# Local attention of the gate stage in blocks of 64 queries with 128 keys each, a tile of two blocks at a step, and outputs divided by the sums instead of weights

## What is computed

```python
h = shift_token(x)
q, k, v = split(h @ wqkv)                 # 8 heads of 64
q, k = l2norm(q) * qs, l2norm(k) * ksc
q, k = rotary_xpos(q, k)
bq = q.reshape(b, h, w, 64, d) * 8.0
bk, bv = look_around(k), look_around(v)   # the block before and the own: 128 keys
sim = einsum('bhwid,bhwjd->bhwij', bq, bk)
mask = (i < j) | (i > j + 64) | (j == -1)
attn = softmax(where(mask, -max, sim))
out = einsum('bhwij,bhwjd->bhwid', attn, bv)
x = x + out @ wo
h = layernorm(shift_token(x)) * lg + lb
a, g = split(h @ w1 + b1)
x = x + (a * gelu(g)) @ w2 + b2
```

## Time and profile before

| | us |
|---|---|
| median of 3 runs | 5320.43 |
| lowest, highest | 5319.44, 5322.79 |
| the profiled execution | 5323.64 |
| its span, first to last instruction | 5322.3 |
| PE busy in the span | 4695.6 (88%) |
| DVE busy | 3288.0 (62%) |
| ACT busy | 2561.0 (48%) |
| POOL busy | 2385.0 (45%) |

### The profile page before, as it was taken

One profiled execution on the slowest core, in us unless ns is written; L12 is line 12 of the kernel. 1 busy time (PEld: TensorE's weight loads), 2 busy tenths in 40 slices (PEclk: granted clock), 3 DMA queues, 4 the chain that ended last, 5 costly groups with the idle time before them and its releaser, 6 DMA issues. The chain is left out here.

```text
span 5322.3 us, 68694 instructions
## 1 busy us (share of the span) xinstructions
PE 4695.6 (88%) x27244; PEld 2291.9 (43%) x27244; DVE 3288.0 (62%) x4302; ACT 2561.0 (48%) x3877; POOL 2385.0 (45%) x1387
## 2 busy tenths in 40 slices
PE   5999999978888688876979999996799999999997
PEld 3444444435556333332423222222445555555554
DVE  4756565637777677684067777855266655655564
ACT  2344444446665355553236666661244444444443
POOL 0455555557666177784010000000046666666675
PEclk8999999989999799897979999997799999999998
DMA  0000000010000000000000000000000000000000
GB/s 32 3 3 3 3 3 4 1 36 9 9 9 1 3 1 2 2 1 23 0 4 1 2 1 2 1 1 8 9 3 3 1 3 3 3 2 2 3 1 9
DMA packets 52289, 27.81 MB, mean 5 GB/s; under 512 B 30036, under 2 KB 48256, under 8 KB 51712
## 3 DMA queue, kind: packets, MB, share of 16 engines
q1 hardware_dynamic: 51968, 23.42, 1.7%
HBM read 22.36 MB, written 1.05 MB: 4 GB/s over the span
## 5 line engine op out<-in xcount | busy, mean ns | idle before, releaser
L793 DVE TENSOR_REDUCE L_part<-banks 128x2 f32<-128x1024 f32 (+2 forms) x1600 | 1882.3, 1190 | 996.4 <-PE banks L644 856.1
L778 ACT ACTIVATE L_weights<-banks 128x1024 f32<-128x1024 f32 (+1 forms) x1600 | 1580.4, 1000 | 1051.5 <-PE banks L676 837.9
L702 PE MATMUL banks<-L_weights,L_V 128*32 128x512 f32 (+3 forms) x6400 | 1500.9, 605 | 5.1 <-ACT L_weights L778 3.0
L1000 POOL TENSOR_TENSOR L_wsum<-L_wsum,L_weights 128x1024 f32<-128x1024 f32 (+1 forms) x448 | 987.2, 2204 | 55.2 <-ACT L_weights L778 2.5
L983 POOL TENSOR_TENSOR L_wsum<-L_wsum,L_two 128x1024 f32<-128x1024 f32 x240 | 570.4, 2377 | 859.1 <-DVE L_two L967 856.3
L702 PEld LDWEIGHTS banks<-L_weights,L_V 128*64 128x64 f32 (+1 forms) x6400 | 283.7, 123 | 460.0 <-issue 397.9
L676 PE MATMUL banks<-L_QH,L_KH 64*128 64x512 f32 (+3 forms) x1664 | 432.2, 453 | 18.1 <-issue 10.2
L2488 POOL MEMSET F_xr<- 128x16 f32 x1 | 0.1, 125 | 932.5 <-POOLq L97 932.5
L644 PE MATMUL banks<-L_KH,L_QH 64*128 64x512 f32 (+3 forms) x1664 | 371.0, 428 | 30.4 <-ACT L_weights L778 17.4
L676 PE MATMUL banks<-L_QL,L_KH 64*128 64x512 f32 (+3 forms) x1664 | 372.3, 382 | 0.0
L676 PE MATMUL banks<-L_QM,L_onesrow 64*128 64x512 f32 (+3 forms) x1664 | 371.6, 381 | 0.0
(11 more groups left out here) (447 smaller groups left out, 6375.9 us busy)
## 6 DMA issues: line engine op xcount, KB each, us to landing
F_tab<-xpos SPq DMA_DIRECT2D x8, 512.0 KB, 4.0
F_h<-L_ffn_h_w SPq DMA_DIRECT2D x2, 1024.0 KB, 7.0
F_wqkv<-L_ffn_wqkv SPq DMA_DIRECT2D x2, 768.0 KB
L_cos<-rope_cos SPq DMA_DIRECT2D x1, 1024.0 KB, 5.0
L_sin<-rope_sin SPq DMA_DIRECT2D x1, 1024.0 KB, 7.1
...
```

What stands on the lines that cost most here:

```text
L702: mm = pe.e.matmul(O[r, c:BANK], self.V[g % 2][:, kt, h, :], self.W[x % self.NW][:, y, c:BANK], start=kt < starts, stop=kt >= tiles - starts)
L778: act.e.activation(self.W[x % self.NW][:, :, c:BANK], self.banks(it)[:, :, c:BANK], ACT.Exp, scale=self.scale).then_inc(self.exped, 1)
L793: dve.e.tensor_reduce(self.part[n % 3][:, pr, j, p, :], self.banks(it)[:, :, 0:wide], AX.X, ALU.max).then_inc(self.mx_read, 1)
L1000: pool.e.tensor_tensor(acc[:, :, c:BANK], acc[:, :, c:BANK], W[:, :, c:BANK], ALU.add).then_inc(self.summed, 1)
```

## The change

A tile's attention is now one step of two half steps, for all eight heads. A tile holds two blocks of 64 queries, and each block is multiplied with its own 128 keys only, so that a score tile has 128 columns of keys for each head instead of 256. The tile of scores has the same two banks, now for 8 heads.

- score: the mask is 128 by 128, read four times over for each bank (2 matmuls a tile instead of 4). The scores are 16 matmuls a tile, each of 64 rows by 64 columns of weights with 128 keys streamed; before they were 8 with 128 columns of weights and 256 streamed.
- exp: 8 exponentials of 128 columns a tile, instead of 8 of 256.
- wturn: 8 transposes a tile instead of 16, straight from the undivided weights.
- values: 16 matmuls a tile as before, 64 weight columns, 64 streamed instead of 128, with no accumulation. The first block's keys straddle two tiles of values, so SP copies them into a tile of their own, early, by two DMAs a tile (63 in all).
- The division: DVE inverts the 8 sums (invert). PE spreads them over 64 rows each by 8 matmuls against the identity (over), which takes one more place in the ring of three banks. ACT copies that to ov. DVE multiplies the outputs in bank 4 with it into oT. ACT's copy of the outputs and the divisions on DVE and POOL are gone.
- The order: the tables are new (one line of two of them is shown), root and norm go to the end of a half step, the layernorm and the norms (now lengths) into the next one, shift goes behind the other items of its half step, exponentials and transposes stand at the first half step and invert, score, over and values at the second.

```diff
-    SPINS = [(-5, 0, 1), (-4, 0, 0), (-3, 1, 1), (-2, 1, 0), (-1, 2, 1), (0, 2, 0), (1, 3, 1), (2, 3, 0)]
...
+    SPINS = [(-8, 0, 0), (-7, 1, 0), (-6, 0, 1), (-5, 1, 1), (-4, 2, 0), (-3, 2, 1), (-2, 3, 0), (-1, 3, 1)]
+    TURNS = [(-4, 0), (-2, 1), (0, 2), (2, 3)]
...
         whole = lambda w: 0 <= w < self.STEPS
         for s in range(min(at), max(at) + 1):
+            w, late = s // 2, s % 2
             rest = sorted(at.get(s, []), key=lambda it: rank[it[0]])
-            cut = (len(rest) + 1) // 2
-            items += [("exp", s + 1)] * whole(s + 1) + [("wturn", s)] * whole(s) + rest[:cut]
-            items += [("divide", s + 1)] * whole(s + 1) + [("score", s + 2)] * whole(s + 2) + rest[cut:] + [("values", s)] * whole(s)
+            if late:
+                items += [("invert", w + 1)] * whole(w + 1) + [("score", w + 2)] * whole(w + 2) + rest + [("over", w), ("values", w)] * whole(w)
+            else:
+                items += [("exp", w + 1)] * whole(w + 1) + [("wturn", w)] * whole(w) + rest
...
+    def early_values(self, sp, t):
+        early, loaded = self.early[t % 2], self.early_loaded[t % 2]
+        self.yread(sp, ("qkv", t // 4, t % 4, 2))
+        if t >= 2:
+            sp.wait_ge(self.pv, t - 1)
+        sp.e.dma_start(early[64:P, :], self.V[t % 8][0:64, :]).then_inc(loaded, 16)
+        if t:
+            sp.e.dma_start(early[0:64, :], self.V[(t - 1) % 8][64:P, :]).then_inc(loaded, 16)
...
+        mask = self.mask[:, min(t % 16, 1), :, :].to_broadcast([P, 4, P])
         for y in range(2):
-            pe.e.matmul(self.buffer(w)[:, y * BANK:(y + 1) * BANK], self.core.identb[:, :], mask, start=True, stop=False)
-        for p in range(2):
-            j = h // 2 + p
-            for y in range(2):
-                r, out = slice(64 * y, 64 * y + 64), self.buffer(w)[:, y * BANK + 256 * p:y * BANK + 256 * p + 256]
-                m = pe.e.matmul(out, self.qT[(4 * u + i) % 3][r, j, :], self.kT[u % 2][r, j, i * P:(i + 2) * P], start=False, stop=p == 1)
+            pe.e.matmul(self.buffer(t)[:, y * BANK:(y + 1) * BANK], self.core.identb[:, :], mask, start=True, stop=False)
+        for j in range(4):
+            for x in range(2):
+                q, k = slice(64 * x, 64 * x + 64), slice(64 + i * P + 64 * x, 64 + i * P + 64 * x + P)
+                for y in range(2):
+                    r = slice(64 * y, 64 * y + 64)
+                    m = pe.e.matmul(self.buffer(t)[q, y * BANK + j * P:y * BANK + (j + 1) * P], self.qT[t % 3][r, j, q], self.kT[u % 2][r, j, k], start=False, stop=j == 3)
         m.then_inc(self.s_made, 1)
...
-    def wturn(self, pe, w):
-        pe.wait_ge(self.by_pool, w + 1)
-        pe.wait_ge(self.by_dve, w + 1)
-        for x in range(8):
-            m = pe.e.transpose(self.buffer(w)[:, x * P:(x + 1) * P], self.wts[w % 2][:, x // 2, x % 2 * P:(x % 2 + 1) * P], self.core.ident[:, :])
+    def wturn(self, pe, t):
+        pe.wait_ge(self.expd, t + 1)
+        for h in range(8):
+            m = pe.e.transpose(self.buffer(t)[:, h * P:(h + 1) * P], self.wts[t % 2][:, h, :], self.core.ident[:, :])
         m.then_inc(self.w_turned, 1)
-    def values(self, pe, w):
...
+    def over(self, pe, it):
+        t = it[1]
+        Y = self.take(pe, it)
+        pe.wait_ge(self.den_made, t + 1)
+        for h in range(8):
+            y, j = h % 2, h // 2
+            m = pe.e.matmul(Y[64 * y:64 * y + 64, j * P:(j + 1) * P], self.rden[t % 2][:, h:h + 1].to_broadcast([P, 64]), self.core.ident[:, :], start=True, stop=True)
+        m.then_inc(self.y_made, 1)
+    def values(self, pe, t):
...
-        for p in range(2):
-            j = h // 2 + p
-            for k in range(2):
-                V = self.V[(t - 1 + k) % 8]
+        pe.wait_ge(self.early_loaded[t % 2], 32 * (t // 2 + 1) - (0 if t % 2 else 16))
+        pe.wait_ge(self.scaled, t)
+        for j in range(4):
+            for x, V in enumerate((self.early[t % 2], self.V[t % 8])):
                 for y in range(2):
-                    a = (h + 2 * p + y) * 64
-                    m = pe.e.matmul(O[64 * y:64 * y + 64, j * P:(j + 1) * P], V[:, a:a + 64], self.wT[w % 2][:, 4 * p + 2 * y + k, :], start=k == 0, stop=k == 1)
+                    h = 2 * j + y
+                    m = pe.e.matmul(O[64 * y:64 * y + 64, j * P + 64 * x:j * P + 64 * x + 64], V[:, h * 64:h * 64 + 64], self.wT[t % 2][:, h, 64 * x:64 * x + 64], start=True, stop=True)
         m.then_inc(self.pv, 1)
...
-            elif kind == "values":
-                if it[1] % 2:
-                    t = it[1] // 2
-                    act.wait_ge(self.pv, it[1] + 1)
-                    if t >= 2:
-                        self.ymade(act, ("join", (t - 2) // 4, (t - 2) % 4))
-                    act.e.activation(self.oT[t % 2][:, :], self.core.bank(4), ACT.Copy).then_inc(self.o_read, 1)
+            elif kind == "over":
+                self.ymade(act, it)
+                act.wait_ge(self.scaled, it[1])
+                act.e.activation(self.ov[:, :], self.ybanked(it), ACT.Copy).then_inc(self.y_act, 1)
...
+        for h in range(8):
+            a = (h % 2) * BANK + h // 2 * P
+            m = act.e.activation(self.wts[t % 2][:, h, :], self.buffer(t)[:, a:a + P], ACT.Exp, bias=self.nm[t % 2][:, h:h + 1],
+                                 scale=self.ssq[u % 2][:, 2, i, 0, h:h + 1], accum_out=self.den[t % 2][:, h:h + 1])
...
-            elif kind == "divide":
-                self.divide(dve, it[1])
+            elif kind == "invert":
+                t = it[1]
+                dve.wait_ge(self.expd, t + 1)
+                if t >= 2:
+                    self.ymade(dve, ("over", t - 2))
+                dve.e.reciprocal(self.rden[t % 2][:, :], self.den[t % 2][:, :]).then_inc(self.den_made, 1)
+            elif kind == "values":
+                t = it[1]
+                dve.wait_ge(self.pv, t + 1)
+                self.yread(dve, ("over", t))
+                if t >= 2:
+                    self.ymade(dve, ("join", (t - 2) // 4, (t - 2) % 4))
+                dve.e.tensor_tensor(self.oT[t % 2][:, :], self.core.bank(4), self.ov[:, :], ALU.mult).then_inc(self.scaled, 1)
...
-    def divide(self, dve, w):
-        rden = self.rden[w % 2]
-        dve.wait_ge(self.expd, w + 1)
-        dve.e.reciprocal(rden[:, :], self.den[w % 2][:, :]).then_inc(self.den_made, 1)
-        dve.wait_ge(self.den_made, w + 1)
-        for x in (2, 3):
-            m = dve.e.tensor_scalar(self.wts[w % 2][:, x, :], self.wts[w % 2][:, x, :], rden[:, x:x + 1], None, ALU.mult)
-        m.then_inc(self.by_dve, 1)
...
-            if kind == "divide":
-                w = it[1]
-                over = self.rden[w % 2][:, 0:2].rearrange("p (h a) -> p h a", a=1).to_broadcast([P, 2, 256])
-                pool.wait_ge(self.den_made, w + 1)
-                pool.e.tensor_tensor(self.wts[w % 2][:, 0:2, :], self.wts[w % 2][:, 0:2, :], over, ALU.mult).then_inc(self.by_pool, 1)
```

139 lines of the change are left out of this document (65 added, 74 removed).

## The result

| | before | after |
|---|---|---|
| median, us | 5321.61 | 5224.72 |
| lowest, highest | 5319.44, 5324.06 | 5224.34, 5225.82 |
| ratio, 95% interval | | 0.9818 (0.9801 to 0.9835) |

The change takes 97 us off. The prediction was 5277, with a range from 5225 to 5315: the sign was right, the size too small by half.

A forecast was written before the change was run, and what follows sets the result against it. It took PE (TensorE) as the bound, with 8.9 us idle a unit. Six units gave -30, first tiles and last unit -9.7 and -2.9: -42.6 in all, 5277 us predicted, range 5225 to 5315.

The forecast's parts named there:

- The price of scores and values: PE's matmuls: values stay at 64 ns a record, 2.05 us a tile (no gain); scores take 2.2 us a tile.
- -11.5: PE's work over 32 tiles: masks, transposes, "over", values and scores sum to -0.36 us a tile, -11.5 us.
- the bound of +59: Upper bound on PE's work change over 32 tiles, in us, if score records cost 138 ns each.
- the slower rival: Score matmuls on PE: quarters don't overlap, each record pays its weight load, 143 ns; +76 us, 5353; chance 0.13.
- the four quarters run at once: Score matmuls on PE: scores and perhaps values halve; priced by scores alone, -37 us, 5240; chance 0.12.
- The walk through the waits: One unit, engine by engine: PE waits 5.3 us instead of 8.9, mainly 3.3 and 1.5 us on ACT.
- 21.6 and 9.7: Idle time saved on PE: 3.6 us in each of six units, and 9.7 us in first tiles and last unit.
- the slow stretch: PE's low clock after its long wait once a unit: expected to remain; were it gone, 2.5 us more a unit.
- The stop: PE's 7.35 us wait before a projection, once a unit, on DVE's row shift behind layernorm, norms and division; expected gone.
- ACT at every step by slow exponentials: ACT's exponentials stay 0.56 us apart, so PE waits 0.9 us more each tile; +28 us, 5305; chance 0.15.
- late early values: SP's early value loads: if two transfers took a step, each tile waits 2 us or more; 5341; chance 0.05.
- a wait that comes in every tile: One of two stated ways the forecast would be wrong, besides a longer group of quarters; no size given.

The follow-up runs named there:

- e4: Changed kernel with its score matmuls reordered so that only two row halves of the array alternate, never four quarters: 5238.8 us.
- e5: Changed kernel with its score matmuls reordered to four in a row on one quarter of the array before the next: 5266.6 us.
- e10: Changed kernel with the prediction's prices put back: score matmuls four in a row on one quarter, values streaming 128 columns (outputs partly wrong): 5265.6 us.
- e9: Kernel before the change with the row shift moved first in the half step with the norms, once a unit: 5315.1 us.
- e12: Kernel before the change with the division of weights left out (outputs undivided): 5286.5 us.
- e13: Kernel before the change with both the division left out and the row shift first in the half step with the norms: 5278.4 us.
- e3: Changed kernel with values matmuls streaming 128 columns instead of 64 (outputs wrong in half their columns): 5214.1 us.
- e1: Changed kernel with four of a tile's eight exponentials on ACT moved behind its copies of turned keys and queries: 5190.3 us.
- e11: Changed kernel with exponentials behind ACT's copies (four ahead in the gelu half step) and DVE's output-projection addition ahead of layernorm and lengths: 5169.3 us.

## Why the prediction was wrong in its size

**The price of scores and values is the step that failed.** The prediction took 64 ns a record "again" for the values, from a row of two halves with 128 streamed columns, and 2.2 us (69 ns a record) for the scores, and thought the weight load was behind it. It had written down the other reading ("if only the streamed columns counted it would be 1.02 a tile") and measured, it is 1.03; scores are 1.03 against 2.2. Together 2.19 us a tile, 70 us. Add 3 for "over" (0.93 against 1.02) to its own -11.5, and PE's work should fall by 84. The balance says 84.1: busy less slow share, 465.5 before, 381.4 after. This agrees better than it should, since part of the slow share falls on idle time. With the low clock counted under PE's busy time alone it is 481.4 and 387.1, 94.3 less. Masks (0.53), transposes of weights (0.93) and the corrected prices hold in the timeline; up to 10 us of PE's fall lies outside the parts that were priced, and no run shows where.

The trace of the kernel before could have told. The values' single records start in pairs there, 6 to 7 ns apart, and the next pair 109 ns after; the transposes of weights, with the whole array, start one at a time, 109 ns apart. Two records 7 ns apart can't each have cost 64 ns of one queue or a weight load of 143; a price per 128 streamed columns of a round fits all three forms. The 138 ns row, which stands behind the bound of +59 and speaks for the slower rival, was misread as well. Its 8.8 us are busy time: 32 pairs that show as some 270 ns each, with modelled ends. From the start of such a pair to the next records it is about 112 ns, 56 a record.

**The rival that came true is the first, "the four quarters run at once"**, to which the prediction gave 0.12. Scores and values both halved, the values by their columns. It was priced by the scores alone at 5240. With both it would have been 5207, and the changed kernel took 5224.7.

The sentence of the Trainium skill that the prediction weighed (TensorE: Matmul & The Clock Gate, section "Wait — 56ns, not 53.3ns?", about 62 ns of sequencer time for each matmul without hardware decode) can't be the price in these runs: a record takes 32 and 29 ns here, and no run shows which way of decoding was on. The same section also says that starts never come closer than about 25 ns. No average here goes below that, but single records on different parts of the array start 6 to 7 ns apart; the measurement decides. The prediction quoted only the sentence that fitted its row. What the Trainium skill says in TensorEngine Tiling (Array Packing), "Key Properties", that tiles load and multiply in parallel, is borne out by e4 and e5.

**What the price would have brought, it didn't bring in full.** The rival with four quarters was priced at -37 us, for scores alone; e5 shows that the order alone is worth 42. From e10 to the changed kernel the two prices fall by 2.28 us a tile (4.34 to 2.06), 73 us, and the median by 41. The balance shows where the others went: idle time is 25.2 higher in the changed kernel (87.9 against 62.7) and the slow share 12.1 higher. PE came sooner to banks that ACT frees, and waited.

**The walk through the waits was right.** At the forecast's prices, in e10, a unit has

```profile
1332.65 0.66 PE L1734 MATMUL banks<-ident,GATE 128*128 128x128 f32 x4 [0.17 <-ACT F_kT L1921]
1348.59 2.50 PE L1709 MATMUL banks<-F_wqkv,F_hT 128*128 128x512 f32 x4 [3.31 <-ACT F_kT L1921]
1362.91 2.84 PE L1724 MATMUL banks<-F_zT,F_w 128*128 128x512 f32 x6 [0.17 <-ACT F_kT L1921]
1381.80 1.13 PE L1709 MATMUL banks<-F_wqkv,F_hT 128*128 128x512 f32 x2 [1.59 <-ACT F_kT L1921]
```

5.24 us in all where the prediction had 5.3, with 3.3 and 1.5 for the two long ones. In the 3.31 us wait both sides of its sum are a little shorter than forecast, PE's 5.6 us instead of 5.8 and ACT's 8.9 instead of 9.1 (the two small roots take 0.25 and not 0.5), so the difference is right by its parts. Idle time of the stage fell by 33.2 from before to e10; the prediction's terms were 21.6 and 9.7. In the changed kernel the waits are 8.3 us a unit, for the reason above. Exponentials stand 0.43 apart (0.45 forecast).

**The clock was sized wrongly.** I kept the slow stretch whole. Its share fell by 19.8 us from before to e10 in the profiled execution, which is 8 us faster than that kernel's median, so the typical share may be some 12. Of the six waits of 3.2 to 3.3 us in e10, three were followed by low clock and three were not; the five stops of 7.35 to 7.7 us before the change all were. The way from the forecast (5277) to e10's 5265.6 is 11 us, about this. But with the low clock counted under PE's busy time alone the fall is 10.4 in that execution, and PE's work falls by as much more; so how much of the 11 us is the clock stays open. In the changed kernel the slow share fell by 7.7 only: the waits of 3.41 us all end in low clock there, and three of the six of 2.40.

**The stop** was put down to a queue in the wrong order with a division in it. e9, e12 and e13 show that order is worth 8 us of time and the division 37. Of these 37 only 13.1 are the stop itself (39.3 to 26.2), 10.0 are waits on divided weights elsewhere, and the clock has a part too. The chain root, layernorm, norms holds PE for 4 us even with both.

Of the other rivals, costly quarters, ACT at every step by slow exponentials, and late early values are all refuted by rows. That ACT would hold PE in each step came true in a way, through a faster PE: the prediction's own sign of being wrong, "a wait that comes in every tile".

## What to carry over

When matmuls fill a part of the array, price a round of one record on each part by its streamed columns, once (here 109 ns for 128 float32 columns, 59 for 64), and order them so that parts alternate. Before taking a weight load or a cost per record for the price, look at the starts of single records. Then ask at each wait whether the saved work lies between the point that starts the releaser's chain and the bank that it frees: saved there, it only lengthens the wait. Put what frees a bank ahead of what nobody waits for in each queue, and look for the next in line after each move.

## What the runs showed of the chip beyond what was expected

- 32 records of 64 rows by 64 columns, 128 streamed: 1.03, 1.52 or 2.50 us, by whether four, two or mostly one quarter of the array is in turn; weight loads of 133 ns each (143 in the stage's mean) were hidden in all three. Single records start 6 to 7 ns apart within a round, rounds about 109 ns apart.
- Records of 64 weight columns in two halves: 29 ns each with 64 streamed columns (eight groups of four, 0.12 apart), 55 with 128 (0.22 apart).
- More work needn't make a kernel slower: 26 us more on PE came with 10.6 us less time (e3), idle time 25.1 lower and slow share 10.2 lower. The clock fell to 1.2 GHz after three of six waits of 2.40 us in the changed kernel, after none of six of 1.59 in e3, and after five of seven of 1.65 in e1.
- Without waits above 1.1 us a whole unit ran at a granted clock of 1.00 (e11). The stage lost 46.9 us to the clock before the change and 11.1 in e11.
